# Bucket 0 given 24 fixed looks among the fills, f's tiles routed one by one with two groups of rows picked by one-hot products, and x1 added by GpSimd during f's leaves

## The reference

```python
for _ in range(DEPTH):                       # 8 decisions lead to one of 256 leaves
    logit = jnp.einsum('bsd,bsd->bs', x, nw[node]) + nb[node]
    node = 2 * node + 1 + (logit > 0).astype(jnp.int32)
leaf = node - NN
h = act(jnp.einsum('bsd,bsdl->bsl', x, w1[leaf]) + b1[leaf])
return jnp.einsum('bsl,bsld->bsd', h, w2[leaf]) + b2[leaf]
...
y = xn + jnp.einsum('bqk,bkd->bqd', att, v)
return y + _fff(y, f_nw, f_nb, f_w1, f_b1, f_w2, f_b2, gelu)
...
x = x + (the feed-forward part of layernorm(x))   # x on the right is x1 below
xn = _layernorm(x)                                # of x2, then layer 1
```

## Time and profile before

| | |
|---|---|
| median of 3 runs | 2539.58 us |
| profiled execution | 2533.6 us, of which the span 2531.8 us |
| PE busy | 2365.1 us, 93% of the span |
| DVE busy | 1405.5 us, 56% |
| ACT, POOL busy | 848.2 us, 268.4 us |
| mean granted TensorE clock | 0.971 |
| chain that ended last | PE 81%, DVE 10%, DMA 4% |

### The profile page before, as it was taken

The page is one execution under the profiler, slowest core; times in us unless marked ns, Lnnn a source line. Parts: engine busy times, 40 slices in busy tenths (PEclk is TensorE's granted clock), DMA queues, the critical chain, the costliest instruction groups (busy, mean ns, idle before and its releaser), DMA issues.

```text
span 2531.8 us, 30996 instructions
## 1 busy us (share of the span) xinstructions
PE 2365.1 (93%) x11841; PEld 1908.6 (75%) x11841; DVE 1405.5 (56%) x2399; ACT 848.2 (34%) x1052; POOL 268.4 (11%) x243
## 2 busy tenths in 40 slices
PE   6899999999999999999899999986959999998998
PEld 4788887777777777777777777875747779876666
DVE  7786353233333333445689886635864323548876
ACT  3132231121121211121267776623843123233442
POOL 3000320000000000010111111002121100202000
PEclk9999999999999999999999999997979999998999
DMA  4255733532132321233788999767874322344884
GB/s 144 55 137 133 150 91 98 133 100 75 52 91 59 92 74 52 62 120 116 273 289 308 356 347 293 255 183 218 314 252 120 107 75 69 107 148 141 315 279 143
DMA packets 168012, 406.67 MB, mean 161 GB/s; under 512 B 69491, under 2 KB 69781, under 8 KB 167837
## 3 DMA queue, kind: packets, MB, share of 16 engines
q1 hardware_dynamic: 145054, 343.04, 42.2%
q0 software_dynamic: 17008, 47.45, 6.4%
q10 hardware_dynamic: 5774, 13.81, 2.0%
HBM read 360.49 MB, written 56.76 MB: 165 GB/s over the span
## 4 chain that ended last, share of the span: by engine, by line
PE 81%; DVE 10%; DMA 4%; issue 3%; ACT 2%; DVEq 0%; SPq 0%; ACTq 0%; POOL 0%; POOLq 0%
PE PS L308 17%; PE PS L309 16%; PE PS L310 16%; PE PS L1145 7%; PE PS L921 4%; PE PS L563 2%; DVE low L300 2%; PE PS L1435 2%; PE PS L1806 2%; PE PS L3035 2%; PE PS L1813 2%; PE PS L1815 2%; PE PS L1814 2%; PE PS L2251 1%; PE PS L327 1%
## 5 line engine op out<-in xcount | busy, mean ns | idle before, releaser
L300 DVE TENSOR_TENSOR low<-raw,high 128x1024 fp32r<-128x1024 f32 x467 | 566.4, 1252 | 127.2 <-ACT high L288 124.2
L288 ACT ACTIVATE high<-raw 128x1024 fp32r<-128x1024 f32 x476 | 484.0, 1056 | 312.5 <-PE PS L310 238.3
L308 PE MATMUL PS<-high,xt_high 128*125 128x512 f32 x1280 | 518.6, 405 | 29.2 <-DVE xt_low L336 10.9
L309 PE MATMUL PS<-low,xt_high 128*125 128x512 f32 x1280 | 511.7, 400 | 0.0
L310 PE MATMUL PS<-high,xt_low 128*125 128x512 f32 x1280 | 510.1, 399 | 0.0
L308 PEld LDWEIGHTS PS<-high,xt_high 128*125 128x125 f32 x1280 | 241.7, 189 | 92.9 <-DVE xt_low L336 12.1
L310 PEld LDWEIGHTS PS<-high,xt_low 128*125 128x125 f32 x1280 | 241.0, 188 | 62.6
L309 PEld LDWEIGHTS PS<-low,xt_high 128*125 128x125 f32 x1280 | 241.8, 189 | 57.9
L1169 ACT ACTIVATE y_high<-PS 125x512 fp32r<-125x512 f32 x80 | 47.8, 598 | 507.9 <-PE PS L310 507.9
L1180 DVE TENSOR_TENSOR y_low<-PS,y_high 125x512 fp32r<-125x512 f32 x80 | 55.3, 692 | 291.6 <-ACT y_high L1169 291.6
L1145 PE MATMUL PS<-y_high,a_kind 125*125 125x512 f32 x400 | 158.4, 396 | 0.0
(11 more groups left out here) (516 smaller groups left out, 3889.0 us busy)
## 6 DMA issues: line engine op xcount, KB each, us to landing
raw<-in_L_ffn_ew SPq DMA_DIRECT2D x96, 512.0 KB
raw<-in_L_gnn_weight SPq DMA_DIRECT2D x64, 512.0 KB
raw<-in_L_ffn_k_w SPq DMA_DIRECT2D x64, 512.0 KB, 7.7
raw<-in_L_ffn_q_w SPq DMA_DIRECT2D x64, 512.0 KB
raw<-in_L_ffn_v_w SPq DMA_DIRECT2D x64, 512.0 KB
raw<-in_L_ffn_f_w SPq DMA_DIRECT2D x64, 512.0 KB, 6.2
adjacency<-a_stage SPq DMA_DIRECT2D x10, 1120.0 KB
a_kind<-adjacency POOLq DMA_DIRECT2D x8, 1367.2 KB, 8.5
```

Of the source, the lines that this page charges most:

```text
L288: a.e.activation(high_of(i)[:, 0:w], RAW[PLACE_OF[i]][:, 0:w], ACT.Copy).then_inc(*a.step(part_high, 1, [("high", i)]))
L300: v.e.tensor_tensor(LOW[p][:, 0:w], RAW[p][:, 0:w], high_of(i)[:, 0:w], ALU.subtract).then_inc(*v.step(signal, 1, [("low", i)]))
L308: p.e.matmul(dst, xh[:, kt, xs], wh[:, c], start=first and j == 0, stop=False)
L309: p.e.matmul(dst, xh[:, kt, xs], wl[:, c], start=False, stop=False)
```

## The change

Four things change.

1. **Start.** Tiles 0 and 1 of x are normalised together, before fill 0; their two fills run interleaved, part by part as the weight parts arrive. ACT normalises tiles 2 to 4. GpSimd no longer splits parts 0 to 5; DVE does.
2. **Bucket 0** has LOOK0 = 24 fixed looks, and behind every fourth stands a half fill (halves 12 to 17). The loop of rounds is left for what is over 24. The other buckets keep four looks and a half fill.
3. **Routing of f.** Leaf numbers, groups and ranks are found tile by tile (`groups_f`, `ranks_f_tensor`, `picks`), the first of them while PE still multiplies attention. For groups 24 and 25 the gather and the turn are replaced: DVE writes one-hot matrices (`PICK`), and PE multiplies the rows of y with them (`pick_tensor`: ten times 8 products of 128 columns), which gives the turned rows in PSUM. All x1 adds move into f's leaves, one per group, with their loads issued by GpSimd.
4. **End of f.** The rows of group 31 are not scattered: they stay in SBUF (`YKEPT`), zeros are scattered in their place before the rows of group 30, and PE adds them to x2 by a product with a one-hot matrix (`PUT`, `merge`). DVE adds f's rows of tiles 0 to 2, GpSimd those of 3 and 4.

The diff, cut to its core:

```diff
         turn(0)
-        fill(0)
         turn(1)
+        p.wait_ge(at("pads"))
+        for j, part in enumerate(Wk[0]):
+            for n in range(2):
+                p.wait_ge(at("xl", "x", n))
+                ins = rows(p, bank(4 + n)[0:PT, :], XTH, XTL, cols(n), part, (2 * j, 2 * j + 1), j == 0, j == 3)
+                if j == 3:
+                    ins.then_inc(*p.mark("fill", n))
         turn(2)
-        fill(1)
         turn(3)
+        fill(2)
         turn(4)
...
-                n = LOOK * b + k
+            some = LOOK if b else LOOK0
+            for k in range(some):
+                n = first_look(b) + k
                 p.wait_ge(at("one hot", n))
-                look(e, ps, n % 5, k == 0, k == LOOK - 1).then_inc(*p.mark("looked", n))
+                look(e, ps, n % 5, k == 0, k == some - 1).then_inc(*p.mark("looked", n))
+                if b == 0 and k % 4 == 3:
+                    fill_half_tensor(p, *halves(12 + k // 4))
             if not points.counting:
                 r = [p.register(f"bound{i}") for i in range(16)]
...
+            if b:
+                fill_half_tensor(p, *halves(half_after(b)))
+        for c in (57, 58, 59):
+            fill_half_tensor(p, *halves(c))
 
...
-        stats(0, 1)
-        normal(0, 1)
-        stats(1, 3)
+        def shifts(a, b):
+            deviations(v, a, b)
+            v.wait_ge(v.last)
+            e.scalar_tensor_tensor(lnx[:, 1, a:b], lnmv[:, a:b, 0], -1.0, rstd[:, a:b], op0=ALU.mult, op1=ALU.mult).then_inc(*v.mark("x shift", a))
+
+        stats(0, 2)
+        normal(0, 2)
+        low_parts(v, 2)
         low(0)
-        normal(1, 3)
-        stats(3, 5)
         low(1)
+        stats(2, 3)
+        low_parts(v, 3)
+        stats(3, 4)
+        low_parts(v, 4)
+        shifts(2, 4)
+        stats(4, 5)
         low(2)
-        normal(3, 5)
+        shifts(4, 5)
         fill_out_vector(v, 0)
         low(3)
...
                 decide_f(t - 2)
+            if t > 2:
+                ranks_f_tensor(p, t - 3)
         turn_y(4)
+        ranks_f_tensor(p, 2)
         decide_f(3)
         decide_f(4)
-        route_ranks_tensor(p, "f", 1, 4, at("el", 4))
+        ranks_f_tensor(p, 3)
+        for t in range(3):
+            pick_tensor(p, t, 0)
+        pick_tensor(p, 3, 0)
+        ranks_f_tensor(p, 4)
+        pick_tensor(p, 0, 1)
+        pick_tensor(p, 4, 0)
+        totals_f_tensor(p)
+        for t in range(1, TT):
+            pick_tensor(p, t, 1)
         route_tokens_tensor(p, "f", 1, 4)
...
+        def groups_f(t):
+            one, lf = slice(t, t + 1), leaf["f"][:, t:t + 1, 0]
+            leaf_numbers(v, SF16[:, one, :], 1, lf, DOWNF[:, one, :])
+            v.wait_ge(v.last)
+            e.tensor_tensor(H16[:, one, :], thr[0:PT, :].unsqueeze(1).to_broadcast([PT, 1, 9]), bc(lf, 9), ALU.is_le).then_inc(*v.mark())
+            v.wait_ge(v.last)
+            e.tensor_tensor(G16[:, one, :], H16[:, one, 0:8], H16[:, one, 1:9], ALU.subtract).then_inc(*v.mark("groups f", t))
+
+        def picks(t):
+
+            v.wait_ge(at("ranks f", t))
+            e.scalar_tensor_tensor(rank1[:, t, :], bank(4)[0:PT, 8 * t:8 * t + 8], 1.0, G16[:, t, :], op0=ALU.add, op1=ALU.mult).then_inc(*v.mark())
+            v.wait_ge(v.last, at("weights turned", 4))
+            for i in range(2):
+                e.tensor_scalar(PICK[i][:, t, :], iota16[0:PT, 1:129], rank1[:, t, i:i + 1], None, op0=ALU.is_equal).then_inc(*v.mark(*("picks", t) if i else ()))
+
         v.wait_ge(*all_stored("v"))
...
         low_y(4)
+        picks(2)
         right_f(3)
+        groups_f(3)
+        right_f(4)
+        picks(3)
+        groups_f(4)
+        picks(4)
+        lfs = leaf["f"][:, :, 0]
+        e.tensor_tensor(MV[:, 0:TT, 8:16], G16[:, 0:TT, :], bc(lfs, 8), ALU.mult).then_inc(*v.mark())
+        e.tensor_copy(MV[:, 0:TT, 16:24], G16[:, 0:TT, :]).then_inc(*v.mark())
+        e.tensor_tensor(MV[:, 0:TT, 0:8], G16[:, 0:TT, :], bc(tokid[:, :], 8), ALU.mult).then_inc(*v.mark("moving", "f", 0))
+        route_slots_vector(v, "f", 1, 4)
+        v.wait_ge(*attended())
+        leaf_rows_low(v, 24)
         low_parts(v, 324)
-        right_f(4)
-        leaf_numbers(v, SF16[:, :, :], TT, leaf["f"][:, :, 0], DOWNF)
-        route_groups_vector(v, "f", "f", leaf["f"])
-        route_slots_vector(v, "f", 1, 4)
+        leaf_rows_low(v, 25)
         route_rows_vector(v, "f", "f", 4)
+        leaf_mask(v, 24)
         route_more_vector(v, "f", "f", leaf["f"])
 
...
+    def load_x1(g, t):
+        g.wait_ge(at("x1 stored", t), at("x1 added", t - 2) if t > 1 else at("vl", t), g.before(cnt_sem))
+        g.e.dma_start(QA[t % 2][:, :], x1d[t * PT:(t + 1) * PT, :]).then_inc(*g.lands(cnt_sem, "x1 again", t))
+
+    def add_x1(g, t):
+        g.wait_ge(g.last, at("x1 again", t), at("turned", "g", 25), at("att stored", t))
+        g.e.tensor_tensor(X2[:, t, :], X2[:, t, :], QA[t % 2][:, :], ALU.add).then_inc(*g.mark("x1 added", t))
...
         leaves_vector(v, F, attended(), lambda v, u: None, lambda v, u: None)
         v.wait_ge(*used_of(lent(AFTER_K + ROUTED, 369)))
+        v.e.tensor_copy(slot_row[:, :], OUTI["f"][:, 7:8]).then_inc(*v.mark())
+        v.wait_ge(v.last)
+        v.e.tensor_scalar(PUT[:, :], iota16[:, 0:N], slot_row[:, 0:1], None, op0=ALU.is_equal).then_inc(*v.mark("row of slot"))
         more_rounds(v, "f", yd, True)
...
+        i = (n - 1) % 2
+        g.wait_ge(g.last, at("turned", "g", n - 1))
+        g.e.memset(XR[i][:, :], 0.0).then_inc(*g.mark())
+        g.wait_ge(g.last, g.before(sx[i]))
+        g.e.indirect_dma_start(out=yb[f], out_offset=bass.IndirectOffsetOnAxis(ap=OUTI[f][:, group:group + 1], axis=0), in_=XR[i][:, :], in_offset=None,
+                               bounds_check=N - 1, oob_is_err=False).then_inc(*g.lands(sx[i], "rows cleared"))
+
     def leaves_gpsimd(g, run, begun, between):
...
             rows_tile(p, t, Wgnn[h], XTH, XTL, n % 4, "gnn", n)
+
+        def merge(t):
+
+            b = MERGED[t]
+            p.wait_ge(at("y out", 31), at("row of slot"), at("x2", 3) if t == 4 else at("x2", t - 2) if t > 1 else at("right f", 4) if t else at("xl", "g", 31))
+            for h in range(2):
...
+
+        for t in range(3):
+            v.wait_ge(at("x1 added", t), at("f back", t))
+            e.tensor_tensor(X2[:, t, :], X2[:, t, :], XQ[t][:, :], ALU.add).then_inc(*v.mark("f added", t))
+        add_merged(0)
+        add_merged(1)
+        measure(0, 2)
+        shifts(0, 2)
+        add_merged(2)
```

More of the change, by code:

```diff
@@ L627, in edges_scalar @@
         fill_out_scalar(a, 5)
+        for c in range(6):
+            high_parts(a, fill_to(*halves(12 + c)))
+            if c in (3, 5):
+                fill_out_scalar(a, 5 + c // 2)
         for b in range(NB):
@@ L829, in start_gpsimd @@
         e.iota(bsti[:, :], [[128, NB]], base=0, channel_multiplier=0).then_inc(*g.mark())
+        for i, (most, least) in enumerate(((164 - LOOK, 164 - LOOK0), (LOOK, LOOK0))):
+            g.wait_ge(g.last)
+            e.memset(looks[:, i, :], float(most)).then_inc(*g.mark())
+            g.wait_ge(g.last)
+            e.memset(looks[:, i, 0:1], float(least)).then_inc(*g.mark(*("looks",) if i else ()))
         mixer_gpsimd(g, M0)
@@ L1840, in turn, with turn_rows @@
         def turn(n):
-            ps = bank(0, 2).rearrange("p (k c) -> p k c", k=8)
+            if n not in run.picked:
+                turn_rows(n)
+            if n != run.first or n not in run.picked:
+                turn_mask(n)
+        def turn_rows(n):
+            ps = bank(rows_bank(n), 2).rearrange("p (k c) -> p k c", k=8)
             a.wait_ge(at("turned", "g", n))
@@ L1857, in leaves_scalar @@
         a.wait_ge(*before)
+        for n in run.picked:
+            turn_rows(n)
         turn(run.first)
@@ L1861, in leaves_scalar @@
                 parts(n, 0, Wf1[GROUP[n]])
+                if n == run.first and n in run.picked:
+                    turn_mask(n)
                 if run.gelu:
@@ L1910, in leaves_vector @@
         v.wait_ge(*before)
-        mask(run.first)
-        turn(run.first)
+        if run.first not in run.picked:
+            leaf_mask(v, run.first)
+            leaf_rows_low(v, run.first)
         for n in range(run.first, run.end + 1):
             if n + 1 < run.end:
-                mask(n + 1)
+                leaf_mask(v, n + 1)
             if n < run.end:
@@ L1928, in leaves_vector @@
                     e.scalar_tensor_tensor(hm, bank(7).rearrange("p (l w) -> p l w", w=16), 0.0, some, op0=ALU.max, op1=ALU.mult).then_inc(*v.mark("hidden", n))
-            if n + 1 < run.end:
-                turn(n + 1)
+            if n + 1 < run.end and n + 1 not in run.picked:
+                leaf_rows_low(v, n + 1)
             within(v, n - run.first)
@@ L1941, in leaves_gpsimd @@
             u = n - run.first
-            if u:
+            if n == run.kept:
+                clear_rows(g, n)
+            if u and n - 1 != run.kept:
```

(4 more changed lines are left out.)

324 lines of the change are left out of this document (196 added, 128 removed).

## The result

The changed kernel takes 2544.5 us (median of 20 runs; 2537.2 to 2549.0), the kernel before 2538.9 (20 runs): a ratio of 1.0021, with a 95% interval from 1.0014 to 1.0028. It is 0.2% slower, where I had forecast 2521 us. The profiled execution took 2540.1 us, 6.5 more than the one of before (span 2538.3 against 2531.8).

A forecast was written before the change was run, and what follows sets the result against it. PE was taken as the bound, busy in most of the span, so only stages where it stands still could give time. Terms -19 + 5.5 + 2 - 7 = -18.5 took 2539.6 to 2521 us; 8 times in 10 between 2510 and 2533.

The forecast's parts named there:

- Start and bucket 0: First stage, up to the end of bucket 0 at 89.7 us: 19 us gained, bounds 12 and 24.
- nothing would be given back there: Behind bucket 0: PE is busy throughout up to the mixer, so none of the 19 us gain is lost.
- Routing: Routing of f up to its first groups: net 5.5 us slower, bounds 8 gained and 9 lost.
- 80 products of 128 float32 columns at the rate of 9.10 us for 80 of 130 columns: Routing of f: the one-hot picks on PE would take 9 us in all.
- The wait that I did forecast: Before group 24's bias product: PE idle for more than 10 us, ended by the mask's copy behind the bias rows.
- the mark: 'routed f', which the weight parts ahead of the bias rows wait for: at 1744.1, 7 us later than before.
- my bound of 9: Routing's worst case: 9 us lost if gathers 26 and 27, issued beside the parts, hold the bias rows up more.
- Adds of x1: f's leaves, five GpSimd adds, one per group: 0.4 us each for the excess, 2 us slower, bounds 0 and 7.
- an upper bound of 7: f's leaves: 7 us lost if every add can block a low part's subtraction, 1.3 us each plus clearing 128 rows.
- My rival on this lock: f's leaves: GpSimd's adds lock DVE, 5.3 us each, 26.5 for five, so 2539.6 us or more; chance 0.02.
- One sign of being wrong that I had named: f's leaves: the forecast is wrong if groups of f take over 14 us.
- End of f: From f's last products into layer 1: 7 us gained, bounds 3 and 12; first turn 15 to 18 us behind.

The follow-up runs named there:

- start_only: The kernel before with only the change's start and bucket 0 parts: 2524.5 us against 2536.1 for the kernel before.
- bias_first: The changed kernel with the bias rows of groups 24 and 26 asked for ahead of the four weight parts: 2525.9 us against 2536.1 for the kernel before.
- picks_half: The changed kernel with 40 instead of 80 one-hot products: 2534.4 us against 2538.9 for the kernel before.
- adds_thin: The changed kernel with GpSimd adding only 8 of 1024 columns of x1 in each add: ratio 1.0001 to the kernel before.
- adds_in_leaves: start_end_bias_first plus the change's loads and five GpSimd adds of x1 in f's leaves: 2524.9 us against 2512.3 for best_again.
- start_end: The kernel before with the change's start, bucket 0 and end of f, without one-hot routing or moved adds: 2517.3 us against 2536.1 for the kernel before.
- start_end_bias_first: start_end with the bias rows asked for ahead of the weight parts: 2512.8 us against 2538.9 for the kernel before.
- best_again: start_end_bias_first run again unchanged, on one chip with adds_in_leaves: 2512.3 us, ratio 0.9897 to the kernel before.

## Why the prediction was wrong

- **Start and bucket 0, -19 forecast, -15.1 measured.** Right in kind: PE waits 4.3 us for DVE at 35.4 us, as said, bucket 0 took 28 looks, and its work ran from 65.36 to 92.1 us, 26.7 us, where I had 27.2. It began 3 us later than I had it. The term is 4 us too large, and start_only shows that it lasts. Of the 4 us, 2.4 are there at the end of bucket 0 (92.1, forecast 89.7). Another 1.6 went in buckets 1 to 4: bucket 1 begins at 92.12 against 94.96 before, bucket 5 at 120.18 against 121.46. I had said that nothing would be given back there.
- **Routing, +5.5 forecast, +17.8 measured: the first step that failed.** What failed is the price of "80 products of 128 float32 columns at the rate of 9.10 us for 80 of 130 columns". The x80 of the earlier trace rows counts records, and each whole-float32 product leaves two of 0.114 us: the loop there makes 40 products. A product of 130 columns costs 0.23 us, four times the 0.060 of split columns. I had weighed the rule of the Trainium skill, "FP8 and Floating Point Precision", section "TensorE Precision Notes" (whole float32 is four passes), against that row and decided for the row; the trace agrees with the rule, with 18.6 us for 80 products, and my reading of the row was wrong. The wait that I did forecast, PE held for more than 10 us by the bias rows, is there, and bias_first shows that it is all of the loss: without it the routing costs nothing. By the links: the forecast had the mark at 1744.1 and the bias product at 1762 in the time of before, 6.6 late (the 5.5 counts 1.1 won behind it). The mark, the last step of the routing on DVE, came at 1740.2; with the lead of 12.6 us added that is 1752.8, 8.7 later than forecast. From the mark to the landing it took 16.7 us instead of 14.0, and the rest 3.7 instead of 3.9: 11.2 together, and 6.6 + 11.2 = 17.8. The price (18.6 - 9.0 = 9.6) is more than the late mark needs; picks_half took 8.9 of it away and got 7.0 back in R. Why the transfer took 2.7 us longer is open: gathers 26 and 27 go beside it, as my bound of 9 had feared, but no run took them away.
- **Adds of x1, +2 forecast (bounds 0 and 7), +10.4 measured: the second failed step.** I took "0.4 us each for the excess" from two adds that together cost 2.6. Only one of these had held DVE: the mask step of 2.43 in the earlier trace rows. Beside the other, from about 1758.5, DVE subtracted rows in PSUM, and no such instruction is held beside an add of x1 in these traces. The held low part beside the third add of before (4.53 us for two) I did not use. In later groups an add falls among low parts and masks, whose inputs both lie in SBUF (the leaf mask, once held, has one), and holds one for 3.0 us as a rule, more than the 1.8 us that a group has to spare. The rule of the Trainium skill, "SBUF — State Buffer", section "Who interferes with whom", says that a DVE instruction with two inputs in SBUF and a GpSimd instruction that reads SBUF contend, and I had used it for an upper bound of 7, at 1.3 an add. On PE an add costs 2.1 us here (10.4 / 5), 2.3 by adds_thin (11.5 / 5) and 1.6 by adds_in_leaves (8.0 / 5); on DVE about 3. My rival on this lock, with 5.3 us an add, had the mechanism, and I gave it 0.02. Its bar was too high even by my own sum: 18.5 + 2 = 20.5 us of gain are gone at 4.1 us an add. One sign of being wrong that I had named, groups of over 14 us, is there in five groups.
- **End of f, -7 forecast, -8.8 measured; first turn 16.9 us behind, 15 to 18 said.** Right; start_end has 7.7 (83.0 against 90.7).

The four measured steps give -15.1 + 17.8 + 10.4 - 8.8 = +4.3, and with +2.5 and -0.5 between them the +6.3 of the last product. With both failed prices right, my own sum would have been 9.6 + 8.4 us higher, 2539: no change. The mechanisms were named; what was missing was to ask of each row what one record of it is, and what the engine beside was reading.

## What to carry to other kernels

Check how many program instructions a count in a trace stands for before a rate is made of it; the loop in the source is next to it. Before an engine is given spare work because it is idle, look at which instructions of the neighbour will run at that time: both inputs in SBUF, and the whole excess of a held one, not the mean over held and unheld ones, is the price of one held instruction. And when a mark moves, walk down the queue behind it: small loads that need no mark belong in front of the large ones that do. This was worth 15 us in the changed kernel for one moved line, and 1 to 3 us where the gather was in the way.

## What the runs showed of the hardware

- A GpSimd add of 125x1024 float32 (2.45 us) holds one DVE instruction in each of 15 cases (five adds in the changed kernel, bias_first and adds_in_leaves): twelve times for 3.0 to 3.2 us more than its like, otherwise 2.8, 2.7 and 2.1. picks_half adds five more, four of 3.0 to 3.2 and one of 2.8. With adds of 8 columns (0.56 to 0.87 us; adds_thin) none is held. The held instruction can be one that would have been over just before the add's record begins: in adds_in_leaves the mask step of 1778.75 + 0.69 = 1779.44 is held, and the add stands at 1779.57. The starts of POOL's records are rough, so which came first is open. In the changed kernel and in picks_half the fifth held one was a leaf mask, with a single float16 input and a column.
- A GpSimd gather issued just ahead of the add can show 3.74 us in place of 1.50 (1796.76 in the changed kernel), while DVE's low parts beside it take their usual 1.2 us (3.49 for three from 1796.11).
- Executions of one program differ in where the granted clock falls. From the first product with the adjacency to the end, the twelve profiled executions of this case take 574.0 to 585.4 us for nearly the same work, by and large the less the higher the clock is there: the three of 574.0 and 574.1 have 0.98, and the one of 585.4 has 0.96. start_end_bias_first and best_again are the same program; from there on the one takes 574.1 us, the other 582.6 (clock 0.98 and 0.97), and their spans differ by 7.7 us (2505.9 and 2513.6), while the medians agree within 0.5. The time of a single profiled execution is good to some 10 us only; its stages say more.
